# A fused DiT block on one NeuronCore: first layer norm's tile turned by VectorE and a DRAM round trip, gates computed as rows, and the instruction order rewritten

## What is computed

```python
m = silu(cond) @ w_ada + b_ada        # nine tables per batch: shift, scale, gate for each of three stages
h = ln(x)*(1+sc_msa)+sh_msa           # A: attention inside windows of 128 rows, the sequence rolled by 64
x = x + g_msa * (window_attention(h) @ w_so + b_so)
h = ln(x)*(1+sc_mca)+sh_mca           # B: cross attention to 77 context rows, only the 16 largest scores kept
x = x + g_mca * (topk_attention(h, ctx) @ w_co + b_co)
h = ln(x)*(1+sc_mlp)+sh_mlp           # C: SwiGLU, hidden size 1024
x = x + g_mlp * ((silu(h@w_m1[:, :1024]+b)*(h@w_m1[:, 1024:]+b)) @ w_m2 + b_m2)
xq, xkv = ada_ln(x, cond), ada_ln(ctx, cond)
out = x + softmax(q(xq) @ k(xkv).T / 4) @ v(xkv) @ Wp + bp    # D: plain cross attention
```

## Time and profile before

| | before |
|---|---|
| median of 3 runs | 1026.23 us (1023.97 to 1029.4) |
| the profiled execution, its own time | 1025.22 us |
| its span, first to last instruction | 1023.4 us |
| mean granted TensorE clock | 0.984 |
| TensorE busy | 975.6 us, 95% of the span |
| VectorE busy | 843.6 us, 82% |
| ScalarE busy | 779.4 us, 76% |
| GpSimd busy | 697.2 us, 68% |

### The profile page before, as it was taken

The page is one execution under the profiler, slowest core; times in us unless marked ns, Lnnn a source line. Parts: engine busy times, 40 slices in busy tenths (PEclk is TensorE's granted clock), DMA queues, the critical chain, the costliest instruction groups (busy, mean ns, idle before and its releaser), DMA issues.

```text
span 1023.4 us, 33174 instructions
## 1 busy us (share of the span) xinstructions
PE 975.6 (95%) x10980; PEld 863.1 (84%) x10980; DVE 843.6 (82%) x4240; ACT 779.4 (76%) x1679; POOL 697.2 (68%) x1093
## 2 busy tenths in 40 slices
PE   5886999999999999999999999999999999999996
PEld 5574788899988889899888888889998988988884
DVE  2348999988998898888898898888999889889644
ACT  2234778788888888888888888888888888887764
POOL 1048556877777777777777777777777777766853
PEclk9887999999999999999999999999999999999999
DMA  8064000000000000000000000000000000000000
GB/s 299 14 143 67 7 8 1 13 12 13 12 13 12 13 7 8 12 13 12 13 13 12 13 11 4 13 12 12 12 12 13 12 13 8 7 7 8 7 7 17
DMA packets 33993, 23.15 MB, mean 23 GB/s; under 512 B 22995, under 2 KB 31443, under 8 KB 33184
## 3 DMA queue, kind: packets, MB, share of 16 engines
q1 hardware_dynamic: 33824, 21.02, 8.1%
HBM read 16.19 MB, written 4.83 MB: 21 GB/s over the span
## 4 chain that ended last, share of the span: by engine, by line
PE 87%; DVE 4%; issue 3%; ACT 2%; POOL 2%; DMA 1%; SPq 0%; POOLq 0%; DVEq 0%; ACTq 0%
PE ps L2137 21%; PE ps L2148 10%; PE ps L2013 8%; PE ps L2126 8%; PE ps L2115 7%; PE ps L2099 7%; PE ps L2085 4%; PE ps L2044 3%; PE ps L2061 3%; PE ps L2024 3%; PE ps L2074 3%; PE ps L2002 2%; PE ps L2034 2%; PE ps L1943 2%; PE ps L1973 1%
## 5 line engine op out<-in xcount | busy, mean ns | idle before, releaser
L2137 PE MATMUL ps<-hT_C,w_m_sb 128*128 128x128 f32 x2048 | 250.4, 276 | 0.4 <-ACT pT_B L859 0.3
L2137 PEld LDWEIGHTS ps<-hT_C,w_m_sb 128*128 128x128 f32 x2048 | 241.2, 192 | 3.7 <-issue 1.4
L866 ACT ACTIVATE silu_C<-ps,cols_sb 128x128 f32<-128x128 f32 x256 | 91.1, 367 | 74.4 <-PE ps L2137 73.0
L2148 PE MATMUL ps<-w_m_sb,hidden_C 128*128 128x256 f32 x512 | 120.7, 379 | 0.0
L538 POOL TENSOR_TENSOR p_B<-p_B,rc_B 128x616 f32<-128x616 f32 x64 | 77.7, 1216 | 62.0 <-DVE p_B L1401 61.0
L1393 DVE MATCH_REPLACE8 scores_left_B<-mx_B,scores_left_B 128x77 f32<-128x77 f32 x512 | 108.3, 224 | 0.0
L1389 DVE MATCH_REPLACE8 scores_left_B<-mx_B,scores_B 128x77 f32<-128x77 f32 x512 | 107.8, 224 | 0.0
L2148 PEld LDWEIGHTS ps<-w_m_sb,hidden_C 128*128 128x128 f32 x512 | 94.6, 190 | 11.4
L1483 DVE SCALAR_TENSOR_TENSOR hidden_C<-ps,cols_sb,silu_C 128x128 f32<-128x128 f32 x256 | 85.2, 343 | 22.6 <-ACT silu_C L866 22.4
L538 POOL TENSOR_TENSOR p_D<-scores_D,rc_D 128x616 f32<-128x616 f32 x63 | 77.0, 1225 | 27.8 <-DVE rc_D L1438 26.9
L1341 DVE TENSOR_REDUCE mx_A<-ps 128x8 f32<-128x1024 f32 x64 | 75.3, 1218 | 17.1 <-PE ps L2044 17.1
(11 more groups left out here) (186 smaller groups left out, 2582.9 us busy)
## 6 DMA issues: line engine op xcount, KB each, us to landing
x_A<-in_x SPq DMA_DIRECT2D x64, 64.0 KB, 2.2
out<-y_D SPq DMA_DIRECT2D x64, 64.0 KB, 2.1
w_m_sb<-in_w_m SPq DMA_DIRECT2D x3, 1024.0 KB, 5.8
w_mod_sb<-in_w_mod SPq DMA_DIRECT2D x2, 1024.0 KB, 11.4
w_qkv_sb<-in_w_qkv SPq DMA_DIRECT2D x1, 768.0 KB, 6.9
w_gate_sb<-in_w_gate SPq DMA_DIRECT2D x1, 768.0 KB, 7.4
rows_sb<-in_rows SPq DMA_DIRECT2D x1, 768.0 KB, 8.7
w_mod_sb<-in_w_mod SPq DMA_DIRECT2D x1, 512.0 KB, 4.1
```

Of the source, the lines that this page charges most:

```text
L866: sc.activation(SA[:, j, :], bank(f"C.up{j}")[:, 0:P], ACT.Silu, bias=col("bm1_a", j)).then_inc(sa_ok, 1)
L2137: ins = mm(bank(f"C.up{j}")[:, half * P:(half + 1) * P], w_m1[:, k, m:m + P], HT["C"][:, t % HT_COPIES["C"], k, :], start=(k == 0), stop=( ...
L2148: ins = mm(bank("C.dn0")[:, 0:CH], G[:, t % G_COPIES, j, :], w_m2[:, j, :], start=(j == 0), stop=(j == HJ - 1))
```

## The change

1. **Stage A's tile is turned without TensorE**, for all tiles but the first. VectorE's new `turn_input` turns `xn_A` in 32x32 blocks into `xn_blocks_A`. SyncE's new `move_input` writes the blocks to a DRAM tensor in four transfers of 32 partitions, in pieces of 32 floats (128 bytes), waits until they have landed, and reads the turned tile back into `xn_A` in one transfer. `modulate` then reads `xn_A` in SBUF instead of PSUM.
2. **Gates as rows.** TensorE multiplies the 4 columns of silu(cond) with the gate weights, giving 4 rows (one for each batch) of 768 channels in PSUM. The bias rows come out as 4 rows too. VectorE forms `gate_rows` and `bias_rows`, SyncE writes them to the DRAM tensor `row_tables`, and reads them back broadcast to 128 partitions, one stage at a time. `screp`, GpSimd's `set_up_gates`, and the 128-partition loads of `rows` and `bp_row` are gone.
3. **The order of all five engines** is a new one in `fill`, `body` and `drain`, as are the tables `BANK` and `LATE_PLACES`; `th`, `q` and `PV` may now take a late bank as well.

```diff
+            def move_input(t):                                   # SyncE
+                sp.wait_ge(xb_ok, t)
+                for i in range(ROWS):
+                    sp.dma_start(turned[t % 2, :, :, :, i, :].rearrange("j k c q -> k c j q"),
+                                 XB[quad(i), :].rearrange("k (c j q) -> k c j q", c=KC, j=ROWS)).then_inc(xb_out, 16)
+                sp.wait_ge(xb_out, 16 * ROWS * t)
+                sp.dma_start(XN["A"][:], turned[t % 2].rearrange("j k c i q -> (j k) (c i q)")).then_inc(xt_in, 16)
...
+            def write_tables():
+                sp.wait_ge(gate_done, 1)
+                sp.dma_start(tables[0, 0:3].rearrange("n b c -> b n c"), gate_rows[:]).then_inc(tables_out, 16)
+                sp.wait_ge(gb_done, 2)
+                sp.dma_start(tables[0, 3:6].rearrange("n b c -> b n c"), bias_rows[:, 0:3, :]).then_inc(tables_out, 16)
+                sp.dma_start(tables[0, 6, 0:1], bias_rows[0:1, 3, :]).then_inc(tables_out, 16)
...
+            def read_tables(s):
+                if s == 0:
+                    sp.wait_ge(tables_out, 16 * 3)
+                spread(gate_mlp[:] if s == 2 else gate[:, s], s, s)
+                spread(gate_b[:, s], 3 + s, s)
...
             def fill():                                          # SyncE
+                write_tables()
+                read_tables(0)
+                move_input(1)
                 load_next_x(2)
+                load_next_x(3)
                 set_up_flat("B", 0)
-                load_next_x(3)
                 set_up_flat("B", 1)
+                load_context_weights()
+                move_input(2)
+                read_tables(1)
+                set_up_flat("D", 0)
                 load_mlp_weights(0)
+                set_up_flat("D", 1)
                 load_next_x(4)
-                load_mlp_weights(1)
-                load_context_weights()
-                set_up_flat("D", 0)
-                load_mlp_weights(2)
-                set_up_flat("D", 1)
+                move_input(3)
                 load_next_x(5)
                 load_next_x(6)
+                load_mlp_weights(1)
+                read_tables(2)
+                load_mlp_weights(2)
...
             def body(i):                                         # SyncE
+                run(store_y, i, 9)
                 run(load_next_x, i, 0)
-                run(store_y, i, 9)
+                run(move_input, i, 1)
...
             def normalise(t, s):                                 # ScalarE
-                    act.wait_ge(h_ps[s], t)
+                    if s == "A":
+                        act.wait_ge(h_ok["A"], t)
+                    else:
+                        act.wait_ge(h_ps[s], t)
...
             def modulate(t, s):
-                act.wait_ge(h_ps[s], t + 1)
+                by_transfer = s == "A" and not first(t)
+                if by_transfer:
+                    act.wait_ge(xt_in, 16 * t)
+                else:
+                    act.wait_ge(h_ps[s], t + 1)
...
+            def turn_input(t):                                   # VectorE
+                dve.wait_ge(xn_ok["A"], t + 1)
+                if t > 1:
+                    dve.wait_ge(xb_out, 16 * ROWS * (t - 1))
+                v.transpose(XB[:], XN["A"][:]).then_inc(xb_ok, 1)
...
+            def set_up_gates():                                  # TensorE
+                for m, (lo, hi) in enumerate(((0, 2 * CH), (2 * CH, 3 * CH))):
+                    for c in range(KC):
+                        ins = mm(ps[0:BATCH, m, 0:hi - lo], scT[:, c, :], w_gate[:, c, lo:hi], start=(c == 0), stop=(c == KC - 1))
```

More of the change, by code:

```diff
@@ L1108, in drain @@
-            def drain():
+            def drain():
+                output_t(TILES - 4, "B")
+                silu(TILES - 5, 0)
+                silu(TILES - 5, 1)
+                silu(TILES - 5, 2)
+                weights_t(TILES - 7, "D", 0)
+                silu(TILES - 5, 3)
+                weights_t(TILES - 7, "D", 1)
+                copy_scores(TILES - 6, "D", 0)
+                silu(TILES - 5, 4)
+                silu(TILES - 5, 5)
+                modulate(TILES - 1, "A")
+                copy_scores(TILES - 6, "D", 1)
+                normalise(TILES - 4, "C")
+                silu(TILES - 5, 6)
+                silu(TILES - 5, 7)
+                exponentials(TILES - 3, "B", 0)
+                exponentials(TILES - 3, "B", 1)
+                key_blocks(TILES - 1)
+                top_exponentials(TILES - 3)
+                normalise(TILES - 2, "B")
+                weights_t(TILES - 7, "D", 2)
+                queries(TILES - 1, "A")
+                modulate(TILES - 2, "B")
```

1236 lines of the change are left out of this document (605 added, 631 removed).

## The result

The changed kernel takes 1020.14 us (median of 5, 1018.17 to 1022.96) where the kernel before takes 1026.23: a ratio of 0.9935 [0.9907, 0.9963], or -6.7 us. The forecast was 1006, with 995 to 1018. So the sign was right, and the gain was a third of the 19 us that I added up; the time lies 2 us above the range. The profiled execution takes 1018.24 us, span 1016.4, to be set against the 1023.4 of before.

A forecast was written before the change was run, and what follows sets the result against it. TensorE was taken to bound the 24 steady bodies, VectorE and GpSimd the fill from 75 us. Terms -5.3 - 0.7 - 12.2 - 2 + 1 = -19.2 from 1025.2 gave 1006 us, range 995 to 1018.

The forecast's parts named there:

- Steady, TensorE, -5.3: 24 steady bodies: dropping TensorE's two transposes of xn_A saves 0.22 us each, -5.3 us.
- VectorE at 92%, costed at nothing: Steady bodies: one more block transpose per tile puts VectorE at 26.07 of 28.39 us, covered by TensorE's gapless row.
- Rival B: Steady bodies: VectorE takes over and leaves small holes, 0.4 us per body, +9.6, giving 1016; chance 0.15.
- The transfer: Steady bodies: the turned tile's round trip through DRAM takes 7.5 us, hidden up to 14.8 us, costed at 0.
- the +1 for a wait in ScalarE's list: Fill: ScalarE's list waits a little for tile 2, +1 us.
- Rival A: ScalarE's modulate: the transfer comes late; at 16 us each body takes 1.2 us more, +29, giving 1035; chance 0.07.
- Earlier start, -2: Start of the fill: VectorE's scale table for tile 0 no longer waits behind tile 1's load, -2 us.
- Gates, -12.2: Fill: gate matmuls shrink from 16.0 to 4.0 us and three adds leave the chain; less a new wait, -12.2 us.
- the new wait for stage B's norm: Fill: TensorE now waits 3.4 us for tile 0's stage-B norm, which the third gate product used to cover.
- rival C: Fill: start not won, through w_m1 late in SyncE's queue or TensorE's lower clock for longer, giving 1015; chance 0.16.
- take over: Fill: VectorE and GpSimd take over after the start; from 75 to 100 us busy 20.98 and 22.20 of 25 us.
- Rest of the order, 0: Fill and drain: the new order otherwise cuts no link out, 0 us, from -4 to +3.

The follow-up runs named there:

- e13_gates_steady_turn: Kernel before with gates as rows and the turn moved to VectorE only from tile 8 on; old fill, banks and drain kept: ratio 0.9890.
- e5_gates_only: Kernel before with only the gates as four rows; its order lists and banks kept, turn still on TensorE: ratio 0.9941.
- e10_gates_busy: Kernel before with only the gates as four rows, plus 23 idle matmuls in five holes of its fill before 66 us: ratio 0.9941.
- e14_gates_steady_busy: Kernel before with gates as rows, VectorE's turn from tile 8 on, and 30 idle matmuls in seven holes of the old fill: ratio 0.9902.
- e4_half_select: Changed kernel with half of VectorE's selection of the 16 largest scores left out for tiles 1 to 3: ratio 0.9912.

## Why the prediction was wrong

- **Steady, TensorE, -5.3.** The mechanism and the size were right: 0.21 us a body in `e13_gates_steady_turn`. The new order keeps 0.17 of it, -3.8 over 23 bodies.
- **VectorE at 92%, costed at nothing.** Right: 650.21 of 715 us is 91%, and TensorE is busy 714.79. Rival B did not occur.
- **The transfer.** Right: 7.1 us where I took 7.5, never waited for; the +1 for a wait in ScalarE's list did not come either. The factor of 19 of the Trainium skill ("VectorE: DVE Perf Modes", section "The three transpose paths"), from which I had an estimate of 25 us, is given there for a large innermost stride at the destination, a condition that I had left out; here each piece is a run of 128 bytes, and the 25 us did not come. Rival A's price fell too: 1.6 us past ScalarE's cover cost 0.2 us a body, not 1.2.
- **Earlier start, -2.** Right: TensorE's first projection starts at 12.13 us, at 14.48 before.
- **Gates, -12.2: the step that failed.** Taken alone they gave 6.1 us by the ratio; at tile 1's mark 5.5 (6.9 in `e13_gates_steady_turn`), at tile 8's 4.6 (6.5). The product is as long as forecast (3.8 us in `e5_gates_only`, 4.5 in the changed kernel, 4.6 in `e13_gates_steady_turn`, forecast 4.0), and the new wait for stage B's norm too (3.73, forecast 3.4). Two other readings were wrong. First, I had kept every other step at its old duration; with less for TensorE to do between waits, its clock was at the low level in other places, and five unchanged steps took 5.1 us more in one execution and 2.6 in two others. The side-by-side rows show it, and `e10_gates_busy` took back 2.4 to 3.8 us at tile 1's mark; how much of it reaches the end is not shown. I had named the clock in rival C as a thing that could last longer; it belonged into the sum. Second, I took the three adds out at 3 x 1.2 = 3.6 us, because each stands in the chain; but TensorE had other work beside them and waited for them only 0.55 + 0.40 + 0.21 = 1.16 us (`before`, above). That is 2.4 us too much. With 2.6 it makes 5.0 of the 12.2 - 6.9 = 5.3 us missing at tile 1's mark in `e13_gates_steady_turn`; in `e5_gates_only` it is 7.5 for 6.7 missing.
- **And what is late next after that.** With idle matmuls a load in SyncE's queue held the values of stage D (4.11 us in `e10_gates_busy`, 3.67 in `e14_gates_steady_busy`), and moving it brought the third scores 2 us forward in the old order. That VectorE and GpSimd "take over" from 75 us, as I read the busy shares, is not borne out: neither `e4_half_select` nor the moves of GpSimd's work made tile 8's mark in the changed kernel earlier.
- **Rest of the order, 0: the second step that failed.** Against the old lists the new ones, with the turn in tiles 1 to 7, cost 5.4 us by the ratios (its bound was +3): 1.5 in the bodies, 2 at the end, the rest not placed. I had taken a rewritten list with the same steps as neutral and looked for a link cut out, not for one put in. The gates fell 6.1 us short; with these 5.4 that is 11.5 of the 12.5 us by which the whole gain fell short.
- **Rivals.** C came nearest in its mechanism, and in half of it; by the time alone (1015) it is no nearer than B (1016), which did not occur. Its other half, w_m1 late in the queue, did not happen: the first up step at 118.20 waits for ScalarE's hT_C. The range ended 2 us too early because C and a loss from the order were never allowed together.

Not tried: which link makes the new drain 2 us longer, and the new fill with TensorE's transposes placed by a search rather than by hand.

## To carry to other kernels

Work taken from TensorE in a stretch where it also waits is not won at its length: count another engine's step in the chain only by what TensorE waits for it, allow for the unchanged steps at the lower clock, and fill the holes with idle matmuls before judging. Look at several executions, not only the profiled one: with the same instructions the clock fell in one and not in the other. After a relief, look for what lands next, loads in a queue included; here idle matmuls gave nothing, an earlier load about 2 us, and the two together 5. And price a rewritten order list by itself: put the same edits into the old list once.

## Not expected of the hardware

- TensorE's granted clock fell to 0.5 several times between 25 and 100 us in every kernel without idle matmuls, mostly after it had waited, but at 28.6 us in `e5_gates_only` behind 12 us in which it was busy for 11.68; in `e13_gates_steady_turn`, with the same instructions there, that fall did not come. With 30 to 34 idle matmuls the mean of the stretch was 0.89 to 0.91, with 48 it was 0.98.
- Four VectorE operations on 77x256 took 4.23 us beside GpSimd's products and 1.37 alone. Not every VectorE operation is stretched so: four MAX8 of the selection took 0.66 us beside the same products (70.39 us in the changed kernel) and 0.64 just before them.
- The gate product took 4.5 us once and 9.2 us three times in a row, with a granted clock of 1.00 shown throughout. The first one is thus about twice as slow as those behind it, and the profile does not say why. The same eight records took 3.79 us in `e5_gates_only`.
